# An experts' layer on one core: ScalarE's exponential of the routing behind its evacuation of the turned q and k

## The reference

```python
rw = gating(x)                       # 4096 x 16, softmax over the picked experts
q = einsum('bte,bted->btd', rw, einsum('btc,ecd->bted', x, q_proj))   # k and v alike
scores = where(causal, einsum('bqd,bkd->bqk', q, k) / 8, -inf)
attn = einsum('bqk,bkd->bqd', softmax(scores), v)
mixed = attn[:, :, None, :] * rw[..., None]
x = layernorm(x + einsum('bted,edc->btc', mixed, o_proj))
```

## Time and profile before

| | |
|---|---|
| median of 3 runs | 4634.78 us (4632.2 to 4635.7) |
| the profiled execution | 4627.98 us, span in the trace 4625.9 us |
| PE busy in the span | 4153.1 us, 90% |
| DVE, ACT, POOL busy | 2547.5, 1699.0 and 1743.2 us |
| the experts' layer | from about 3653 us to the end |

### The profile page before, as it was taken

How to read it: one execution, slowest core, us unless ns; L and a number is a source line. 1 busy time by engine, 2 the same in 40 slices (tenths; PEclk the granted TensorE clock), 3 DMA queues, 4 the chain that set the end, 5 groups by cost and what they waited for, 6 DMA issues and landing times. The chain is left out here.

```text
span 4625.9 us, 66773 instructions
## 1 busy us (share of the span) xinstructions
PE 4153.1 (90%) x21492; PEld 2421.7 (52%) x21492; DVE 2547.5 (55%) x4031; ACT 1699.0 (37%) x3116; POOL 1743.2 (38%) x1232
## 2 busy tenths in 40 slices
PE   5899899989999984899989998999999499999998
PEld 3443643454365423644554355436543377777776
DVE  2564455346545633477557655755674455555554
ACT  1354154425534540244335433442344222222222
POOL 2213222412232112276427633762473244444443
PEclk9999999989999997899999999999999699999998
DMA  2221222132223204322332143224220400000000
GB/s 86 63 63 48 79 67 64 49 92 51 51 79 79 59 24 152 77 42 56 114 101 49 49 146 83 42 61 143 67 48 9 148 22 29 33 28 29 28 28 12
DMA packets 136667, 294.91 MB, mean 64 GB/s; under 512 B 19888, under 2 KB 38192, under 8 KB 136304
## 3 DMA queue, kind: packets, MB, share of 16 engines
q1 hardware_dynamic: 125808, 273.07, 21.9%
q10 hardware_dynamic: 10496, 17.31, 1.0%
HBM read 145.87 MB, written 43.25 MB: 41 GB/s over the span
## 5 line engine op out<-in xcount | busy, mean ns | idle before, releaser
L1103 ACT ACTIVATE probs<-half 128x512 f32<-128x512 f32 x2048 | 1112.7, 595 | 1013.7 <-PE half L907 465.7
L904 PE MATMUL half<-stack 97*128 97x512 f32 x2048 | 876.5, 492 | 64.3 <-ACT probs L1103 28.7
L1334 DVE TENSOR_REDUCE mx<-wide 128x1 f32<-128x1024 f32 x512 | 601.9, 1220 | 554.2 <-PE wide L865 547.7
L1330 DVE CUSTOM_DVE_ANT_0 wide<-wide,mask_q 128x1024 f32<-128x1024 f32 x512 | 617.6, 1248 | 279.0 <-PE wide L865 261.7
L865 PE MATMUL wide<-stack 96*128 96x512 f32 x2048 | 652.8, 434 | 90.1 <-DVE mx L1330 39.4
L904 PEld LDWEIGHTS half<-stack 97*128 97x128 f32 x2048 | 374.7, 194 | 675.3 <-ACT probs L1103 318.0
L769 POOL TENSOR_TENSOR psums<-psums,probs 128x1024 f32<-128x1024 f32 x232 | 550.0, 2390 | 157.6 <-ACT probs L1103 138.3
L1720 PE MATMUL work_e<-w_in_e,x_e 128*128 128x512 f32 x2304 | 573.7, 401 | 19.1 <-DVEq L1976 11.3
L848 PE MATMUL acc<-probs,v 128*32 128x512 f32 x4096 | 552.3, 609 | 3.0 <-ACT u L1072 3.0
L865 PEld LDWEIGHTS wide<-stack 96*128 96x128 f32 x2048 | 389.2, 197 | 215.3 <-DVE mx L1330 66.6
L1720 PEld LDWEIGHTS work_e<-w_in_e,x_e 128*128 128x128 f32 x2304 | 429.8, 191 | 120.8 <-issue 20.8
(11 more groups left out here) (235 smaller groups left out, 4753.5 us busy)
## 6 DMA issues: line engine op xcount, KB each, us to landing
stack<-qk SPq DMA_DIRECT2D x336, 256.0 KB, 4.9
y<-x SPq DMA_DIRECT2D x8, 2048.0 KB, 8.7
x<-y SPq DMA_DIRECT2D x8, 2048.0 KB, 7.6
x_t<-xts ACTq DMA_DIRECT2D x16, 1024.0 KB, 6.0
mstage<-mask SPq DMA_DIRECT2D x32, 512.0 KB, 4.4
mstage<-mask_t SPq DMA_DIRECT2D x32, 512.0 KB, 4.1
stage<-x_t SPq DMA_DIRECT2D x24, 512.0 KB, 3.7
stack<-first SPq DMA_DIRECT2D x48, 256.0 KB, 5.0
```

The source lines that it names most:

```text
L904: last = pe.matmul(bank[:, :], stack[0:3 * DH + 1, s, 2 + h, kt * P:(kt + 1) * P], stack[0:3 * DH + 1, s, h, c * CH:(c + 1) * CH], start=T ...
L1103: act.activation(probs[:, kt % 2 * 2 + h, c * CH:(c + 1) * CH], bank[:, :], ACT.Exp, scale=SCALE).then_inc(free, 1)
L1330: dve.tensor_tensor_reduce(bank[:, :], bank[:, :], mask_q[:, t, :], 1.0, -3e38, ALU.add, ALU.max, mx[:, p % 3, n:n + 1]).then_inc(free, 1)
L1334: dve.tensor_reduce(mx[:, p % 3, n:n + 1], bank[:, :], AX.X, ALU.max).then_inc(free, 1)
```

## The change

The step that ACT does for the routing gets a name of its own, pick, and a place of its own in the list: ("pick", now) stands behind ("turn", one), in the slot after. DVE's route(nxt) stays where it was. No instruction is added or removed, and PE, DVE, POOL and SP keep their order; only on ACT the exponential and its table load move behind the next slot's split, square and the two copies of turn.

```diff
@@ token_slot @@
-        ("p", now, 0), ("turn", one), ("out", two), ("p", now, 1),
+        ("p", now, 0), ("turn", one), ("pick", now), ("out", two), ("p", now, 1),
@@ expert_layer, block.scalar @@
-                    elif kind == "route":
+                    elif kind == "pick":
                         act.wait_ge(pick_in, number + 1)
```

## The result

The change is slower: 4654.1 us median against 4632.2 us of the kernel before, ratio 1.0044 (95% interval 1.0031 to 1.0057), some 20 us. Forecast were 4646 us and +11.2. The direction and the first part of the mechanism were right, the size was not, and the time lies 2 us above the range. The 4646 stood on a median of 4634.8 for the kernel before; against the 4632.2 of all its runs the miss is 2.6 us larger.

A forecast was written before the change was run, and what follows sets the result against it. PE was taken as busy in nearly every slice of the experts' layer, so only its gaps count. Slots 7.8, opening 1.9 and DVE's lateness 1.5 made 11.2 us slower: 4646 us, range 4631 to 4652.

The forecast's parts named there:

- The stall that goes: Score's weight load on PE waits for ACT's copies of q and k; 12.6 us outside the opening should go.
- What is late next: PE at prob_t then waits for the scores' exponential; without anything else about 9.2 of 12.6 us come back.
- all of the stall comes back: Rival: prob_t doesn't bind PE either, so the kernel gets faster, 4623.5 us; chance 0.05.
- nothing but the opening moves: Rival: the exponential isn't the last thing on ACT before PE needs it; only the opening's cost shows, 4636 us; chance 0.02.
- What the split brings with it: POOL's half of the split starts during route on DVE and holds L1926 0.93 us longer, 0.7 before tile 6.
- the port does not matter: Rival: POOL's split does not hold DVE; 9.2 us come back against the opening's 1.3, 4627 us; chance 0.15.
- only TENSOR_TENSOR is held: Rival: POOL holds L1932 on DVE, not L1926; delay 0.63 us, about +4 in all, 4639 us; chance 0.13.
- The opening: First slots: the first exponential on ACT moves behind the second tile's split, which waits for its DMA: 1.9 us slower.
- The sum per slot: Experts' layer on PE: per slot the smaller of stall and slack minus delay; together 7.8 us slower.
- The delay of route: On DVE, L1926 and the chain above it end 0.93 us later through POOL's split, 0.7 before tile 6.
- slacks of the prediction: Room between the scores' exponential and PE's load reading it: tile 0 1.20 us, 4 0.73, 5 0.08, 6 0.28, 7 0.03.
- DVE late against PE: Tiles 4 to 7: L2029 waits for POOL's adds as DVE drifts against PE; 0 to 3 us, taken as 1.5.

The follow-up runs named there:

- second profile: The changed kernel run and profiled once more with no edit: 4650.1 us, ratio 1.0041 to the kernel before.
- the reduces: The changed kernel with L2017 and L2029 on DVE as tensor_reduce of two columns instead of two-input instructions: 4642.7 us, ratio 1.0021.

## Why the prediction was right or wrong

What was foreseen and held:
- *The stall that goes.* 12.6 us of waiting for L1848 are gone.
- *What is late next.* PE waits for L1858, in nearly every slot. So the rivals in which all of the stall comes back, or nothing but the opening moves, fall too.
- *What the split brings with it.* L1926 is held by POOL's split; undone by one wait on POOL, the loss vanishes. The rivals in which the port does not matter, or only TENSOR_TENSOR is held, are excluded by L1926's row.
- *The opening.* +1.9 was forecast, 1.0 and 2.5 came (1.2 to 2.0 in the four experiments with this order in the opening); with the exponential ahead of the split it is 0.1.

The steps that failed can be read tile by tile. The numbers are the growth of the distance between one start of mixed_t (L1774) and the next against before, in us, summed over the batches:

| tile | forecast | first profile | second profile |
|---|---|---|---|
| 0 | -0.8 | -0.4 | -0.5 |
| 1 to 3 | 0 | +0.3 | -0.6 |
| 4 | +1.2, and the 1.5 of L2029 | +7.4 | +7.3 |
| 5 | +3.4 | +5.9 | +5.9 |
| 6 | +1.3 | +4.5 | +4.7 |
| 7 | +2.7 | +2.0 | +3.6 |
| opening | +1.9 | +1.0 | +2.5 |
| behind the last mixed_t | 0 | -1.1 | -1.2 |

The +3.6 of tile 7 contains the dip of the closing slot (1.6). Of the -1.1 behind the last mixed_t 0.9 is clock as well: a group of 12 matmuls there took 5.49 us before and 4.61 now.

- **The step that failed is "The sum per slot": it had no price for PE's clock.** It took a wait for its length. In tiles 4 to 7 PE stands at prob_t for 0.4 to 0.8 us per slot, where it stood for nothing before, and behind that it ran p(now, 4) at 1.2 GHz in seven slots, 1.6 us more each, of which a part fills waits that follow. The price can be read from slots of the same tile with and without a dip, as growth against before: 2.14 us against 1.2 in tile 4, 2.13 against 0.73 in tile 5, 1.93 and 2.09 against 0.45 in tile 6. Over the seven slots that makes about 8.4 of the 19.5 us (an estimate; in the last batch the slots without a dip are those of other profiles). A row for it was in the trace of before, where the loop's jump leaves PE standing for 3.6 us:

```profile
3962.81 4.56 PE L1720 MATMUL work_e<-w_in_e,x_e 128*128 128x512 f32 x12 [3.58 <-issue]
```

That is p(now, 0), which takes 3.0 elsewhere. I had read it as a thing of long waits.

- **The delay of route was taken with POOL where it stood.** 0.93 us was worked out from a split that starts at the end of an undisturbed tree. With DVE later, POOL's trees move together and the split starts later against route, and L1898 is held too: in the slot shown 4035.56 + 1.34 is 2.98 us behind L1894, where it was 4021.77 - 4020.04 = 1.73 before, so 1.25 us. That is the largest kind; in the second batch the delay is 1.23 us for tile 4, 0.98 for tile 5, 0.85 for tile 6 and 0.76 for tile 7. With the slacks of the prediction these give 0.90 for tile 5, 0.57 for tile 6 and 0.73 for tile 7, and 0.7 to 0.9, 0.45 and 0.6 to 0.7 came where the clock stayed. For tile 4 they give 0.50, and 1.2 came; the 0.7 between them is gone with the reduces (1.2 becomes 0.5 there), so it is DVE late against PE, below.
- *The sum without the clock* is 19.5 - 8.4 = 11.1 us, against 11.2 forecast. That it fits so well is luck in part: tile 4 lost some 2 us more than its share and tiles 0 to 3 gave back 0.7 less, while the opening cost 0.9 less, tile 7 lost 0.7 less and the close 1.1.
- *DVE late against PE* was put at 1.5 us from L2029. The experiments without the split in route show that it is real, 1.8 us and more in tile 4, and that L2017 is held too, by 0.5, 0.4 and 0.3 us in tiles 5, 6 and 7 and not at all in tile 4, before the change as well. I had read the slacks of 0.03 to 0.28 as given; part of them was POOL's doing.
- The Trainium skill ("ScalarE: Activation LUTs", section "What ACT_TABLE_LOAD costs") adds a drain of 1.38 us to a table load of 1.28. The trace does not agree: the exponential starts 0.01 us behind its load in all 32 slots of the change, as it did before, and ACT stands idle for 0.2 us ahead of the load of the square root (L1831).

## What to carry to other kernels

Before moving a step up on one engine, follow the other engines that it releases: here the moved split cost ACT nothing and let POOL start beside the one stretch on DVE that the next wait hangs on. Where DVE's chain is critical and POOL works beside it, look at the minimum and maximum of small two-input instructions; a spread like that of L2017, from 159 to 690 ns, showed the contention here, and a form with one SBUF input ended it. And when PE gets new short waits, price them with the clock behind them: the row to look at is the same group of matmuls behind a wait and elsewhere.

## What the runs showed of the hardware

- A DVE instruction that reads two SBUF tensors was held to the end of the POOL instruction beside it, SCALAR_TENSOR_TENSOR as well as TENSOR_TENSOR: L1926, 16 columns, took up to 1342 ns in place of 235 and L1898, one column, up to 806 in place of 160. L1926 was held even where the profile has it start 0.01 us ahead of POOL's. A tensor_reduce of two columns beside the same POOL work took 154 to 158 ns.
- In seven slots in which PE stood for 0.4 to 0.8 us at prob_t it had half of its clock behind that, for some 3.5 us. Not always: tile 7 stood 0.7 us in its slots and the clock fell in none of its three in the first profile, but in two of them with the split early and turn late, and tile 4 stood 0.56 us both in a slot with a dip and in one without. What exactly decides was not tried.
- With useless matmuls in the place of such waits no slot of tiles 4 to 7 had a dip behind prob_t, and the layer was 7.3 us shorter in its profile (9.4 against the second profile of the change).
